# Both convolutions of a four-block network: TensorE reads the centre operand in place from X, 192 elements from column to column

## The chip, the cores and the metric

The kernel runs on one core of one Trainium2 chip. The metric is the device time of one execution in microseconds; before the change its median is 4312.59 us over 3 runs (4307.71 to 4313.99).

## The reference

The input is 2 images of 192 channels and 112 x 112 pixels in float32. Four blocks follow one another: window attention with an MLP; a Sobel filter with a 1x1 fusion, a norm over channels and a GELU; a block with a depthwise 7x7 convolution, a norm, an MLP of 768 hidden features with response normalisation, and a residual; and a sum of seven depthwise convolutions, some dilated, each with its batch norm. The kernel folds the last block into one depthwise 13x13 convolution with a bias. The change touches the two depthwise convolutions alone:

```python
# block 3, first step
y = conv_general_dilated(x, dw_w, padding=((3, 3), (3, 3)), feature_group_count=192) + dw_b
# block 4
out = bn(dwconv(x, w_lk, 1))
for i, (w, r) in enumerate(zip(branch_ws, (1, 1, 2, 3, 4, 5))):
    out = out + bn(dwconv(x, w, r))
```

## The kernel before

The whole activation lives in one on-chip tensor `X` of shape [128, NB = 196, C = 192]. A partition is a position in a patch of 8 rows by 16 columns of pixels; the 196 blocks are 2 images x 14 x 7 such patches; the channel is the innermost index. So for a fixed channel the 196 values of a partition lie 192 elements, 768 bytes, apart.

`depthwise` runs twice: as `dw7` after the Sobel stage and as `dw13` at the end. It loops over the 192 channels. For a channel, the convolution becomes matmuls whose stationary operand is a 128 x 128 Toeplitz matrix of taps (`mats`), and whose moving operand is the channel's blocks, one column for each block. A pixel's neighbours lie in its own patch or in patches around it. Six matmuls add up in one PSUM bank: for each of the row offsets 0, -1 and +1 one with the centre operand and one with the operand shifted by half a patch. Offset 0 has 196 columns, the others 182.

Five engines work on a channel, coupled by semaphores and rings of R = 4 buffers:

- SP loads the channel's taps, spread out, from DRAM into `raw` (line 1145, ring of U = 8).
- VectorE (`body`, up to line 1182) waits until the matmuls of four channels before have freed the ring place (`conv`), copies X's channel into the dense tile `xc` (line 1179, signals `xc_ready`), waits for `raw`, and copies it into the first Toeplitz matrix (line 1182, `mats_a`).
- GpSimd copies the shifted operand `xs` in two halves from X, 64 partitions and 168 elements each (line 1165, `xs_ready`).
- ScalarE writes the second Toeplitz matrix (line 1196, `mats_b`) and, two channels behind, adds the bias and moves the result out of PSUM (line 1209): in dw7 back into X at the same channel, in dw13 into a dense tile `res` that a DMA from ScalarE's queue stores.
- TensorE waits for the operands and for the PSUM bank, and issues the six matmuls (line 1232).

`run_steps` writes the first 8 channels out with constant addresses and runs the other 184 in a loop of 8 channels a turn, whose channel number comes from a register. The order on each engine is that of the program; there is no planner.

Of the kernel before, what the change touches and what calls it, by code (L numbers as in the profile page):

```python
# [23 lines left out]
IMG, BY, BX = 2, 14, 7  # L24
# [1085 lines left out]
def depthwise(nc, tag, turn, q, loaded, wide, bias, X, PS, out, expanded, stack):  # L1110
# [4 lines left out]
    s = Scope(nc, tag, stack)  # L1115
    U, HEAD, R, G = 8, 8, 4, 4
    raw = s.sb("raw", [128, U, RUN[turn]])
    mats = s.sb("mats", [128, R, 2, 24, 16])
    xc = s.sb("xc", [128, R, IMG, BY, BX])
    xs = s.sb("xs", [128, R, IMG * BY, BX])  # L1120
    brow = s.sb("brow", [128, C])
    res = s.sb("res", [128, 2, G, NB]) if out is not None else None
# [10 lines left out]
    with nc.Block() as block:  # L1133
        @block.sync
        def _(sp):
            sp.dma_start(brow[:, :], bias.partition_broadcast(128)).then_inc(q["bloaded"], 16)  # L1136
            sp.wait_ge(expanded, 16 * EXPANSIONS)

            def body(t):
                b = t.ahead(first)  # L1140
                if t.reached(U):
                    sp.wait_ge(q["mats_a"], b.n - U + 1)
                    sp.wait_ge(q["mats_b"], b.n - U + 1)
                src = wide[bass.ds(t.n, 1)].rearrange("o p g -> (o p) g")
                sp.dma_start(raw[:, b.buf(U), :], src).then_inc(loaded[b.buf(U)], 16)
            run_steps(sp, C, U, HEAD, 0, body)

        @block.gpsimd
        def _(pool):
            nc.gpsimd.memset(mats[:, :, :, :, :], 0.0).then_inc(q["cleared"], 1)  # L1150
            nc.gpsimd.memset(xs[:, :, :, :], 0.0).then_inc(q["ready"], 1)
            pool.wait_ge(q["ready"], turn + 1)

            def body(t):
                b = t.ahead(first)
                reached = at_hand(pool, b.n - R + 1)
                pool.wait_ge(q["ready"], turn + 1)
                if b.reached(R):
                    pool.wait_ge(q["conv"], reached)
                for h in range(2):  # L1160
                    if h:
                        pool.wait_ge(q["xs_half"], b.n + 1)
                    src = X[64 * h:64 * h + 64, :, bass.ds(t.n, 1)].rearrange("p (y x) o -> p y (x o)", x=BX)
                    dst = xs[64 * h:64 * h + 64, b.buf(R), :, :]
                    last = nc.gpsimd.tensor_copy(dst[:, :, h:h + BX - 1], src[:, :, 1 - h:BX - h])  # L1165
                    if not h:
                        last.then_inc(q["xs_half"], 1)
                last.then_inc(q["xs_ready"], 1)
            run_steps(pool, C, U, HEAD, 0, body)

        @block.vector
        def _(dve):
            dve.wait_ge(q["cleared"], turn + 1)

            def body(t):
                b = t.ahead(first)
                if b.reached(R):
                    dve.wait_ge(q["conv"], b.n - R + 1)
                nc.vector.tensor_copy(xc[:, b.buf(R)].rearrange("p i y x -> p (i y x)"), X[:, :, bass.ds(t.n, 1)].rearrange("p b o -> p (b o)"))\  # L1179
                    .then_inc(q["xc_ready"], 1)  # L1180
                dve.wait_ge(loaded[b.buf(U)], b.turn(U) * 16 + 16)
                nc.vector.tensor_copy(mats[:, b.buf(R), 0, held, :], toeplitz(b, 0)).then_inc(q["mats_a"], 1)  # L1182
            run_steps(dve, C, U, HEAD, 0, body)

        @block.scalar
        def _(act):
            act.wait_ge(q["bloaded"], 16 * (turn + 1))
            act.wait_ge(q["cleared"], turn + 1)

            def body(t):  # L1190
                if t.inside(C):
                    b = t.ahead(first)
                    if b.reached(R):
                        act.wait_ge(q["conv"], b.n - R + 1)
                    act.wait_ge(loaded[b.buf(U)], b.turn(U) * 16 + 16)  # L1195
                    nc.scalar.activation(mats[:, b.buf(R), 1, held, :], toeplitz(b, 1), ACT.Identity).then_inc(q["mats_b"], 1)  # L1196
                c = t.back(2)
                if not c.inside(C):
                    return
                b = c.ahead(first)  # L1200
                act.wait_ge(q["conv"], b.n + 1)
                src = PS[:, b.buf(4), 0:NB]
                if out is None:
                    dst = X[:, :, bass.ds(c.n, 1)].rearrange("p b o -> p (b o)")
                else:
                    dst = res[:, c.buf(2 * G) // G, c.buf(G), :]
                    if c.reached(2 * G) and c.buf(G) == 0:
                        act.wait_ge(stored[c.buf(2 * G) // G], c.turn(2 * G) * 16)
                nc.scalar.activation(dst, src, ACT.Identity, bias=brow[:, bass.ds(c.n, 1)]).then_inc(q["result"], 1)  # L1209
                if out is not None and c.buf(G) == G - 1:  # L1210
                    act.wait_ge(q["result"], b.n + 1)
                    act.dma_start(out[bass.ds(c.n - (G - 1), G)].rearrange("c p b -> p c b"), res[:, c.buf(2 * G) // G]).then_inc(stored[c.buf(2 * G) // G], 16)
            run_steps(act, C, U, HEAD, 2, body)
            if out is not None:
                for j in range(2):
                    act.wait_ge(stored[j], 16 * (C // G // 2))

        @block.tensor
        def _(pe):
            def body(t):  # L1220
                b = t.ahead(first)
                pe.wait_ge(q["xc_ready"], b.n + 1)
                pe.wait_ge(q["xs_ready"], b.n + 1)
                pe.wait_ge(q["mats_a"], b.n + 1)
                pe.wait_ge(q["mats_b"], b.n + 1)
                if b.reached(4):
                    pe.wait_ge(q["result"], b.n - 3)
                src = (xc[:, b.buf(R)], xs[:, b.buf(R)].rearrange("p (i y) x -> p i y x", i=IMG))
                for i, (oy, sh) in enumerate(((0, 0), (0, 1), (-1, 0), (-1, 1), (1, 0), (1, 1))):
                    ylo, yhi = max(0, -oy), BY - max(0, oy)  # L1230
                    m = mats[:, b.buf(R), sh, 8 * (1 - oy):8 * (1 - oy) + 8, :].rearrange("p r c -> p (r c)")
                    last = nc.tensor.matmul(ps(b)[:, :, ylo:yhi, :], m, src[sh][:, :, ylo + oy:yhi + oy, :], start=(i == 0), stop=(i == 5))  # L1232
                last.then_inc(q["conv"], 1)
            run_steps(pe, C, U, HEAD, 0, body)
# [233 lines left out]
def build(nc, a, out):  # L1468
# [10 lines left out]
    with ExitStack() as whole:  # L1479
        whole.enter_context(nc.allow_non_contiguous_dma(reason="vectors of 192 to 768 elements, once"))  # L1480
        X = whole.enter_context(nc.sbuf_tensor("X", [128, NB, C], F32))
        PS = whole.enter_context(nc.psum_tensor("PS", [128, 8, 512], F32))
        expanded = nc.alloc_semaphore("expanded")
        used = nc.snapshot_sems()
        with ExitStack() as stack:
            attention(nc, a, d, X, PS, expanded, stack)
        nc.clear_and_free_semaphores(nc.allocated_since(used))
        nc.all_engine_barrier()
        with ExitStack() as stack:
            mlp(nc, a, d, X, PS, stack)  # L1490
        with ExitStack() as stack:
            sobel(nc, a, d, X, PS, stack)
        sems = Scope(nc, "dw", whole)
        convs = ({x: sems.sem(x) for x in ("bloaded", "ready", "cleared", "mats_a", "mats_b", "xc_ready", "xs_half", "xs_ready", "conv", "result")},
                 sems.sems("loaded", 8))
        with ExitStack() as stack:
            depthwise(nc, "dw7", 0, *convs, d["wide"][0], a["L2_conv_dw_b"], X, PS, None, expanded, stack)
        with ExitStack() as both:
            gain2 = both.enter_context(nc.sbuf_tensor("gain2", [128, IMG, MC, C], F32))
            cvec = both.enter_context(nc.sbuf_tensor("cvec", [128, C], F32))  # L1500
            with nc.sbuf_tensor("ss", [128, NP, MC], F32) as ss:
                with ExitStack() as stack:
                    hidden(nc, a, d, X, PS, ss, stack)
                with ExitStack() as stack:
                    response_norm(nc, a, PS, ss, gain2, cvec, stack)
            with ExitStack() as stack:
                project(nc, a, d, X, PS, gain2, cvec, stack)
        with ExitStack() as stack:
            depthwise(nc, "dw13", 1, *convs, d["wide"][1], d["bias"], X, PS, out, expanded, stack)
# [25 lines left out]
```

## Time and profile before

| what | value |
|---|---|
| median of 3 runs | 4312.59 us |
| the profiled execution | 4318.69 us, its span 4316.8 us |
| mean granted TensorE clock | 0.93 of full speed |
| PE busy | 3693.2 us (86%) |
| VectorE, ScalarE, GpSimd busy | 55%, 42%, 44% |
| dw7's matmuls (line 1232) | from 2749.8 us to about 3117 us |
| dw13's matmuls | from 3945.2 us to the end |

Busy times are summed over the span and hide that the stages differ; slices and windows split them. Two consecutive matmul records overlap in the trace, so the printed duration of one is longer than the distance to the next. In a timeline "x2" means that two records in a row have been put on one line. The column after the second "|" in the groups is the idle time of the engine before the group, with what ended it.

### The profile page before, as it was taken

How to read it: one execution, taken by the hardware profiler on the slowest of the kernel's cores; microseconds unless marked ns; L12 is line 12 of the kernel's file. 1: busy time of each engine (PE TensorE's matmuls, PEld its weight loads, DVE VectorE, ACT ScalarE, POOL GpSimd, SP SyncE). 2: the span in 40 equal slices, each digit the busy share in tenths (PEclk: the TensorE clock that was granted, in tenths of full speed). 3: DMA queues.
4: the chain of work that ended last, by engine and by line, in shares of the span. 5: the costliest groups of instructions: out<-in, count | busy, mean ns of one | idle time of the engine just before them, and what ended most of it. 6: DMA issues, size and time to landing. Idle time of an engine off the chain costs nothing. (4 is left out here: it accounts for less than half of the span.)

```text
span 4316.8 us, 104641 instructions
## 1 busy us (share of the span) xinstructions
PE 3693.2 (86%) x32726; PEld 3544.2 (82%) x32726; DVE 2377.2 (55%) x5922; ACT 1823.7 (42%) x5208; POOL 1902.3 (44%) x2891
## 2 busy tenths in 40 slices
PE   3888888888869999999755555699999989999999
PEld 2777777777769999999755555699989989999999
DVE  2555555556543333333399999544389971113444
ACT  1555555555534444444211122344379960001444
POOL 2222222222213333333499999555434433334555
PEclk9999999989979999999877777899999999999999
DMA  2444566620000000000122322455457778887887
GB/s 62 137 160 161 176 221 211 219 86 19 19 19 20 21 27 27 23 24 27 45 60 75 79 72 72 125 149 149 114 163 199 199 197 253 253 252 241 266 267 228
DMA packets 473876, 551.74 MB, mean 128 GB/s; under 512 B 89875, under 2 KB 343573, under 8 KB 473621
## 3 DMA queue, kind: packets, MB, share of 16 engines
q1 hardware_dynamic: 448276, 528.61, 41.6%
q10 hardware_dynamic: 25344, 19.27, 1.4%
q8 instruction: 216, 3.54, 0.3%
q14 instruction: 40, 0.32, 0.0%
HBM read 408.63 MB, written 271.27 MB: 158 GB/s over the span
## 5 line engine op out<-in xcount | busy, mean ns | idle before, releaser
L1232 PE MATMUL PS<-dw_xc,dw_mats 128*128 128x182 f32 (+1 forms) x2304 | 554.4, 322 | 34.4 <-ACT dw_mats L1196 34.4
L1104 PE MATMUL PS<-sobel_wf,sobel_edge 96*128 96x192 f32 (+1 forms) x1568 | 333.2, 384 | 268.6 <-DVE sobel_edge L1035 234.2
L1165 POOL COPY dw_xs<-X 64x168 f32 (+1 forms) x768 | 426.4, 555 | 300.5 <-PE PS L1232 238.8
L1232 PE MATMUL PS<-dw_xs,dw_mats 128*128 128x182 f32 (+1 forms) x2304 | 553.3, 321 | 0.0
L1104 PEld LDWEIGHTS PS<-sobel_wf,sobel_edge 96*128 96x128 f32 (+1 forms) x1568 | 325.1, 232 | 276.6 <-issue 261.7
L1232 PEld LDWEIGHTS PS<-dw_xc,dw_mats 128*128 128x128 f32 x2304 | 401.5, 190 | 35.0 <-issue 35.0
L880 PE MATMUL PS<-mlp_w,mlp_hid 128*128 128x192 f32 x2352 | 414.2, 326 | 0.5 <-ACT mlp_hid L756 0.5
L1232 PEld LDWEIGHTS PS<-dw_xs,dw_mats 128*128 128x128 f32 x2304 | 401.1, 189 | 0.0
L362 POOL TENSOR_SCALAR att_ve<-att_mv 128x2 f32<-128x2 f32 x98 | 22.5, 229 | 858.9 <-DVE att_mv L409 858.9
L1463 PE MATMUL PS<-gain,down_hid 128*128 128x192 f32 x2352 | 385.5, 328 | 3.8 <-DMA down_hid<-scratch_hid 3.8
L1463 PEld LDWEIGHTS PS<-gain,down_hid 128*128 128x128 f32 x2352 | 385.2, 191 | 4.2 <-DMA down_hid<-scratch_hid 4.2
L880 PEld LDWEIGHTS PS<-mlp_w,mlp_hid 128*128 128x128 f32 x2352 | 378.7, 190 | 0.8 <-ACT mlp_hid L756 0.8
L1179 DVE COPY dw_xc<-X 128x196 f32 (+1 forms) x384 | 149.1, 388 | 392.6 <-PE PS L1232 383.0
L1196 ACT ACTIVATE dw_mats<-dw_raw 128x224 f32<-128x224 f32 (+1 forms) x384 | 163.7, 426 | 453.2 <-DMA dw_raw<-scratch_wide 422.9
L487 ACT ACTIVATE att_vbd<-PS 64x96 f32<-64x96 f32 x784 | 194.7, 248 | 341.7 <-PE PS L596 334.9
L840 DVE TENSOR_TENSOR mlp_x<-PS,X 128x192 f32<-128x192 f32 x196 | 70.2, 358 | 482.0 <-PE PS L880 472.6
L756 ACT ACTIVATE mlp_hid<-PS,mlp_b 128x256 f32<-128x256 f32 x588 | 247.0, 471 | 111.0 <-PE PS L747 111.0
L807 POOL COPY X<-mlp_x 128x192 f32 (+1 forms) x196 | 68.2, 348 | 468.5 <-DVE mlp_x L840 467.5
L756 ACT ACTIVATE hid_hid<-PS,hid_b 128x256 f32<-128x256 f32 x588 | 236.9, 471 | 34.2 <-PE PS L747 34.2
L1451 DVE TENSOR_TENSOR X<-PS,down_x 128x192 f32 (+1 forms) x196 | 70.0, 357 | 319.5 <-PE PS L1463 319.5
L1443 POOL TENSOR_TENSOR down_x<-down_x,cvec 128x192 f32<-128x192 f32 x196 | 115.8, 591 | 271.9 <-DMA down_x<-scratch_x 271.9
L1182 DVE COPY dw_mats<-dw_raw 128x224 f32<-128x224 f32 (+1 forms) x384 | 223.8, 583 | 3.9 <-DMA dw_raw<-scratch_wide 3.6
(218 smaller groups left out, 10379.9 us busy)
## 6 DMA issues: line engine op xcount, KB each, us to landing
scratch_wide<-scratch_taps SPq DMA_DIRECT2D x64, 1188.0 KB, 6.6
dw_raw<-scratch_wide SPq DMA_DIRECT2D x192, 396.0 KB, 4.1
scratch_hid<-hid_hid SPq DMA_DIRECT2D x196, 384.0 KB, 3.6
down_hid<-scratch_hid SPq DMA_DIRECT2D x196, 384.0 KB, 4.1
scratch_wide<-scratch_taps SPq DMA_DIRECT2D x64, 828.0 KB, 5.1
dw_raw<-scratch_wide SPq DMA_DIRECT2D x192, 276.0 KB, 2.8
sobel_xin<-scratch_x SPq DMA_DIRECT2D x56, 420.0 KB, 3.9
att_x<-in_x SPq DMA_DIRECT2D x196, 96.0 KB, 1.9
```

What stands on the lines that cost most here:

```text
L487: last = nc.scalar.activation(vbd[64 * e:64 * e + 64, b.buf(4), w, :, e, 0:HD], src, ACT.Identity)
L756: last = nc.scalar.activation(hid[:, m, :], self.psU[i][:, e * 256:(e + 1) * 256], ACT.Gelu, bias=self.b1[:, m:m + 1])
L840: nc.vector.tensor_tensor(x1[:, b.buf(2), :], psD[b.buf(2)], at(X, b.n), ALU.add).then_inc(q["x1_ready"], 1)
L880: last = nc.tensor.matmul(psD[i], hid[:, p.buf(2), m, i * 128:(i + 1) * 128], w2[:, m, :], start=(m == 0), stop=(m == MC - 1))
L1104: last = nc.tensor.matmul(psF(t, j), edge[0:rows, t.buf(2), e, j, :], wf[0:rows, e, :], start=(e == 0), stop=(e == 2 * KC - 1))
L1165: last = nc.gpsimd.tensor_copy(dst[:, :, h:h + BX - 1], src[:, :, 1 - h:BX - h])
L1179: nc.vector.tensor_copy(xc[:, b.buf(R)].rearrange("p i y x -> p (i y x)"), X[:, :, bass.ds(t.n, 1)].rearrange("p b o -> p (b o)"))\
L1182: nc.vector.tensor_copy(mats[:, b.buf(R), 0, held, :], toeplitz(b, 0)).then_inc(q["mats_a"], 1)
L1196: nc.scalar.activation(mats[:, b.buf(R), 1, held, :], toeplitz(b, 1), ACT.Identity).then_inc(q["mats_b"], 1)
L1232: last = nc.tensor.matmul(ps(b)[:, :, ylo:yhi, :], m, src[sh][:, :, ylo + oy:yhi + oy, :], start=(i == 0), stop=(i == 5))
L1443: nc.gpsimd.tensor_tensor(x2[:, b.buf(R), :], x2[:, b.buf(R), :], cvec[:, :], ALU.add).then_inc(q["resid"], 1)
L1463: last = nc.tensor.matmul(PS[:, b.buf(R), 0:C], hid[:, b.buf(R), m, :], gain2[:, img, m, :], start=(m == 0), stop=(m == MC - 1))
```

## The change

The tile `xc`, VectorE's copy into it and its semaphore are dropped. The moving operand of the three centre matmuls becomes a view of X itself at the channel, in dw7 and dw13 alike. The shifted operand, the Toeplitz matrices, the order of the matmuls and their number of columns stay as they are.

```diff
-    xc = s.sb("xc", [128, R, IMG, BY, BX])
...
                 if b.reached(R):
                     dve.wait_ge(q["conv"], b.n - R + 1)
-                nc.vector.tensor_copy(xc[:, b.buf(R)].rearrange("p i y x -> p (i y x)"), X[:, :, bass.ds(t.n, 1)].rearrange("p b o -> p (b o)"))\
-                    .then_inc(q["xc_ready"], 1)
                 dve.wait_ge(loaded[b.buf(U)], b.turn(U) * 16 + 16)
...
-                pe.wait_ge(q["xc_ready"], b.n + 1)
                 pe.wait_ge(q["xs_ready"], b.n + 1)
...
-                src = (xc[:, b.buf(R)], xs[:, b.buf(R)].rearrange("p (i y) x -> p i y x", i=IMG))
+                centre = X[:, :, bass.ds(t.n, 1)].rearrange("p (i y x) o -> p i y (x o)", i=IMG, y=BY)
+                src = (centre, xs[:, b.buf(R)].rearrange("p (i y) x -> p i y x", i=IMG))
                 for i, (oy, sh) in enumerate(((0, 0), (0, 1), (-1, 0), (-1, 1), (1, 0), (1, 1))):
```

`"xc_ready"` also leaves the list of semaphores in `build`.

## Rows read from the trace of the kernel before

**Rows 1.** Busy us, share and instructions by engine, from the page.
```profile
PE 3693.2 (86%) x32726; PEld 3544.2 (82%) x32726; DVE 2377.2 (55%) x5922; ACT 1823.7 (42%) x5208; POOL 1902.3 (44%) x2891
```

**Rows 2.** The span in 40 slices of 107.9 us, from the page.
```profile
PE   3888888888869999999755555699999989999999
...
PEclk9999999989979999999877777899999999999999
```

**Rows 3.** Windows: us; busy us (count) PE, PEld, DVE, ACT, POOL; clock, DMA, GB/s.
```profile
2775.00:2950.00 175.00, 175.00 (x1108) 175.00 (x1108) 79.47 (x186) 74.30 (x186) 102.41 (x185) 1.00 0.55 149
3945.00:4312.80 367.80, 367.53 (x2304) 367.28 (x2304) 173.89 (x382) 157.18 (x383) 211.16 (x380) 0.99 0.86 260
```

**Rows 4.** Chain that ended last, in order: start us, us, what.
```profile
3939.27 5.14 DMA dw_raw<-scratch_wide
...
3944.51 0.48 ACT dw_mats L1196
...
3945.23 367.54 PE PS L1232 x2304
```

**Rows 5.** Waits in the first convolution: us in total, times, longest.
```profile
DVE dw_xc L1179 <- PE PS L1232: 98.6, 95, 1.0
```

**Rows 6.** Timeline of one channel: start us, us, engine, line, operation, count.
```profile
3002.01 0.49 PE L1232 MATMUL PS<-dw_xc,dw_mats 128*128 128x196 f32 x2
...
3003.30 0.47 PE L1232 MATMUL PS<-dw_xc,dw_mats 128*128 128x182 f32 x2
...
3003.61 0.47 PE L1232 MATMUL PS<-dw_xs,dw_mats 128*128 128x182 f32 x2
...
3003.91 0.49 PE L1232 MATMUL PS<-dw_xc,dw_mats 128*128 128x196 f32 x2
```

**Rows 7.** Groups by line and shape: count, busy us, mean ns.
```profile
L1232 PE MATMUL PS<-dw_xc,dw_mats 128*128 128x182 f32 x1536 | 363.7, 318 | 0.0
```

**Rows 8.** VectorE's two copies: duration ns min/median/max.
```profile
L1179 DVE COPY dw_xc<-X x384: 364/384/770, 2746.9 to 4305.3; 128x196 f32 x184, 128x196 f32<-128x196 f32 x8
...
L1182 DVE COPY dw_mats<-dw_raw x384: 277/569/626, 2749.2 to 4305.6; 128x224 f32<-128x224 f32 x96, 128x320 f32<-128x320 f32 x96
```

**Rows 9.** GpSimd's shifted copy and its register operations, as rows 8.
```profile
L1165 POOL COPY dw_xs<-X x768: 451/477/705, 2747.6 to 4306.2; 64x168 f32 x184, 64x168 f32<-64x168 f32 x8
L1165 POOLq FUSED_REGOPS  x736: 42/46/56, 2761.3 to 4306.1; - x184
```

**Rows 10.** ScalarE's groups, as rows 7: strided, dense, two dense sizes.
```profile
L1209 ACT ACTIVATE X<-PS,dw_brow 128x196 f32 x184 | 111.0, 603 | 201.8 <-PE PS L1232 201.8
...
L1196 ACT ACTIVATE dw_mats<-dw_raw 128x320 f32<-128x320 f32 x192 | 89.0, 464 | 441.9 <-DMA dw_raw<-scratch_wide 411.7 <-ACT dw_res L1209 30.2
...
L1209 ACT ACTIVATE dw_res<-PS,dw_brow 128x196 f32<-128x196 f32 x192 | 81.5, 424 | 179.4 <-PE PS L1232 179.4
...
L1196 ACT ACTIVATE dw_mats<-dw_raw 128x224 f32<-128x224 f32 x192 | 74.7, 389 | 11.2 <-DMA dw_raw<-scratch_wide 11.2
```

**Rows 11.** A dense GpSimd copy, as rows 8.
```profile
L807 POOL COPY X<-mlp_x x196: 342/349/500, 1303.9 to 2120.2; 128x192 f32 x168, 128x192 f32<-128x192 f32 x28
```

**Rows 12.** GpSimd's groups, as rows 7: shifted copy, 6-element copy.
```profile
L1165 POOL COPY dw_xs<-X 64x168 f32 x736 | 409.3, 556 | 289.4 <-PE PS L1232 229.3 <-POOL dw_xs L1165 60.1
...
L1275 POOL COPY ss<-hid_part 128x6 f32 x90 | 17.1, 190 | 120.5 <-DVE hid_squares L1304 120.5
```

**Rows 13.** Timeline of line 747, PE alone, first and last of 14 records.
```profile
3399.73 0.28 PE L747 MATMUL PS<-hid_ha_hi,hid_wa_lo 128*128 128x256 f32 x1
...
3401.24 0.28 PE L747 MATMUL PS<-hid_hb,hid_wb_lo 128*128 128x256 f32 x1
```

**Rows 14.** Timeline of the first convolution's first channel, PE alone.
```profile
2751.24 0.81 PE L1232 MATMUL PS<-dw_xc,dw_mats 128*128 128x182 f32 x2
2751.85 0.81 PE L1232 MATMUL PS<-dw_xs,dw_mats 128*128 128x182 f32 x2
```

**Rows 15.** Window of the stretch of rows 14, columns as rows 3.
```profile
2751.20:2753.00 1.80, 1.80 (x7) 1.80 (x7) 0.84 (x3) 0.00 (x0) 1.16 (x2) 0.50 1.04 406
```

More of the change, by code:

```diff
@@ L1493, in build @@
         sems = Scope(nc, "dw", whole)
-        convs = ({x: sems.sem(x) for x in ("bloaded", "ready", "cleared", "mats_a", "mats_b", "xc_ready", "xs_half", "xs_ready", "conv", "result")},
+        convs = ({x: sems.sem(x) for x in ("bloaded", "ready", "cleared", "mats_a", "mats_b", "xs_half", "xs_ready", "conv", "result")},
                  sems.sems("loaded", 8))
```

## The prediction

> **What bounds the kernel now.** I read first the busy shares of the page: PE is busy 86% of the span, its weight loads (PEld, which overlap) 82%, and no other engine is above 55% [rows 1]. An average over stages says little, so the slices come next: PE stands at 9 in the slices near 2750 to 3113 us and in those from 3945 us to the end, the two convolutions, with PEclk 9 [rows 2]. The windows table makes it exact: in 175 us of the first convolution PE is busy for 175.00 us at granted clock 1.00, while VectorE is busy 79, ScalarE 74 and GpSimd 102 us; the second shows 367.53 of 367.80 us [rows 3]. The chain that ended last agrees: from 3945.23 on it is 367.54 us of line 1232 [rows 4]. The waits show the other side: VectorE's xc copy waits for PE, 98.6 us in 95 times in a like window [rows 5]. Last, the timeline of one channel: centre and shifted matmuls alternate, and a channel takes from 3002.01 to 3003.91, 1.90 us [rows 6]. So TensorE alone sets the pace of both convolutions, and what counts is how long its own matmuls take.
>
> **How the program's matmuls stand in the trace.** A channel has 6 matmuls, 3 of them on the centre operand. Two of the 3 have 182 columns, over 384 channels 768, and the trace has 1536 records of them [rows 7]: each f32 matmul is two records, each with all its columns. A printed duration (318 ns) is not a record's cost, since they overlap; the cost is the spacing. 1108 records in 175 us [rows 3] are 0.158 us each, 12 a channel, 1.895 us. With 186.7 columns in the mean that is 0.85 ns a column. The centre reads per channel are 2 x (196 + 182 + 182) = 1120 columns.
>
> **The change part by part.**
>
> *The copy goes.* 384 copies of 384 ns [rows 8], about 149 us of VectorE. Each begins when PE has freed its ring place and has 98.6/95 = 1.04 us of idle VectorE in front of it [rows 5]; it lies wholly beside the PE of a channel. Worth 0 us. What PE still needs, the shifted copies and both Toeplitz copies, is made up to three channels ahead and comes as early as before or earlier, so nothing is late in its place.
>
> *One wait goes* in front of PE's channel. The spacing from a channel's last pair to the next channel's first is 0.30 to 0.31 us, that inside a channel 0.31 [rows 6]: the five waits that are there now cost nothing visible. I take 0; a bound for the gain is 0.01 us x 384 = 4 us. At the start of each convolution PE's first matmul waits for ScalarE's Toeplitz copy, whose data came by DMA [rows 4], not for xc: 0.
>
> *Addresses from a register.* For 184 of 192 channels the centre matmuls' addresses now depend on the loop counter. The trace shows what that costs GpSimd: one FUSED_REGOPS of 46 ns for each copy of X [rows 9]. PE's form is not shown. If each of the 6 centre records needs one, 6 x 46 = 276 ns of issuing stand beside 1895 ns of streaming and run ahead of it, since the ring has operands ready. I take 0; uncovered, it is 0.276 x 368 = 102 us.
>
> *The read itself.* This is the term that decides. The moving operand was dense in xc; now its consecutive columns lie 192 x 4 = 768 bytes apart. No row shows PE reading so. The nearest rows are of other engines doing the very same walk over X. ScalarE, from the same PSUM source with the same 196 elements, takes 603 ns to write to X and 424 ns to write densely [rows 10]: +179 ns, 0.91 ns an element. Its dense pace is (464 - 389)/(320 - 224) = 0.78 ns [rows 10], so 1.69 ns an element with the step. GpSimd reads X: its dense copy takes 349 ns for 192 elements and 190 for 6, 0.85 ns an element [rows 11, 12]; with the step the median is 477 ns for 168 [rows 9], (477 - 190)/162 = 1.77 ns. VectorE's copy has 384 ns for 196, its dense Toeplitz copy at its quickest 277 for 224 [rows 8]: at least 107 ns more for fewer elements, 0.55 ns each. Three engines, reads and writes, each lose 0.5 to 0.9 ns where neighbours are 768 bytes apart, and two end at 1.7 to 1.8 ns an element. That looks like the pace of the memory for lone words, and PE needs one every 0.85 ns.
> I take 1.69 ns, because its pair of rows differs in nothing but the step. Then a centre column costs 1.69 - 0.85 = 0.84 ns more: 1120 x 0.84 = 0.94 us a channel, 361 us over 384. Low end: nothing, if PE's port has room (below). A gain is excluded, since the columns are the same and there was no gap to close. High end: GpSimd's mean beside other traffic, 556 ns [rows 12], is (556 - 190)/162 = 2.26 ns, so 1.41 x 1120 x 384 = 606 us.
>
> *A rule against the change.* What the rows show is the loss of 0.5 to 0.9 ns an element [rows 8 to 12]. The Trainium skill, "SBUF — State Buffer", section "SBUF: two separate sides", says that the memory is read in lines of 16 bytes and that two hits on a line are needed to hide its latency; "Advanced Engine Details and Errata", "SBUF Cachelines", says that a new line at each access is penalised. By that rule each column of X is a line of its own and the change loses; the three engines of this trace agree in sign. "Vector Engine (DVE) Microarchitecture Reference", "Measured stream behaviour on trn2", gives 0.65 of a VectorE cycle for each lone word, about 0.68 ns; as an estimate from that page the sum would be 1120 x 0.68 x 384 = 292 us. Neither page gives a number for TensorE, and no row here does.
>
> *Sum.* The profiled execution took 4318.7 us (span 4316.8 us, 1.9 us around it), 6.1 us above the median of the runs, 4312.6. On its time: 4318.7 + 361 = 4680; on the median 4674. I put the forecast at 4676. What else touches the time: with a channel of 2.84 us the other engines have more slack; their longest here, GpSimd, is busy 102 of 175 us.
>
> **The rivals.**
>
> *A. The step is free for PE* (not slower). PE's own moving operand is read faster elsewhere: the single-record matmuls of line 747 start 1.51/13 = 0.116 us apart with 256 columns [rows 13], 0.454 ns a column of 4 bytes. An f32 record takes only one column per 0.85 ns. If the step halves that rate, PE gets one per 0.91 ns, which is 0.06 ns late: 1120 x 0.06 x 384 = 26 us at most, and 0 if the 0.454 ns hold some cost per record. Time 4310 to 4340, likeliest 4313. For it: PE can take nearly double what an f32 record asks, while the engines above were at their own pace when dense. Against it: the 0.454 ns is for neighbours side by side, as was ScalarE's 0.78, and that one didn't save ScalarE from 1.69 with the step. It decides if a lone word comes in 0.85 ns or less.
>
> *B. Each record reads each column twice.* 0.85 ns is nearly twice 0.454 ns, so a record may fetch a column for each of two passes. At 1.69 ns a fetch a column takes 3.38 ns: 2.53 x 1120 x 384 = 1088 us, 5400 us. Against it: two passes could use one fetch.
>
> *C. Issuing decides.* The 102 us above in full, with a free read: 4415 us. The first 8 channels of each convolution, whose addresses are constants, would keep 1.895 us while the others don't.
>
> *D. A smaller loss for the step*, by buffering in front of the array: 50 to 230 us, 4360 to 4545.
>
> *E. Faster*: waits gone and one reader of X fewer, at most the 4 us above, 4309; over 0.2% would need something that no row shows.
>
> **How the numbers follow.** Forecast (1.4 to 1.8 ns a column, 4550 to 4760 around 4676): 0.52. A: 0.26. B and other losses above 4770, among them a granted clock that falls while the array is fed slowly (at the lower clock a pair of 182 columns takes 0.61 us, at the full one 0.31 [rows 6, 14, 15]): 0.09. C: 0.03. D: 0.07. E: 0.03. The predicted time is the likeliest, 4676. A has to be inside, so the range runs from 4306 to 4770 and leaves out B and a corner; the forecast's own is 4550 to 4760. What can be told from no change is about 0.2%, 9 us. Of A's 0.26, 0.04 may lie above that. Faster 0.03, same 0.22, slower 0.75.
>
> **What the profile after would show.** The spacing of the line 1232 records that read X against those that read xs is the whole test: about 0.33 us a record of 196 columns under the forecast, 0.165 under A, 0.66 under B; the shifted records keep 0.158. Under the forecast a channel takes 2.84 us, PE still waits for nobody, the idle time in front of ScalarE's activations grows by nearly 1 us, and the second convolution goes from 367.5 us to about 548. VectorE loses 149 us of busy time in every case. All other stages keep their times. The forecast is wrong if the records on X keep the spacing of the others, if only the loop's channels are longer (C), or if the clock falls in the convolutions.

## The result and the profile after

The changed kernel takes 4670.69 us (median of 4 runs, 4665.56 to 4675.08) against 4310.15 us for the kernel before (4 runs): a ratio of 1.0843, 95% interval 1.0813 to 1.0873. It is 360.5 us slower. The forecast was 4676, 5 us above the measured time.

The page's first lines, busy us and instructions by engine, answer to [rows 1]:
```profile
PE 4050.7 (87%) x32726; PEld 3650.3 (78%) x32726; DVE 2153.6 (46%) x5538; ACT 1826.9 (39%) x5208; POOL 1845.5 (39%) x2891
```
PE's busy time grew by 357 us with the same 32726 records. VectorE's fell by 224 us.

A window in the first convolution, columns as [rows 3]:
```profile
2775.00:2950.00 175.00, 175.00 (x739) 134.44 (x738) 17.18 (x62) 51.12 (x124) 59.71 (x124) 1.00 0.36 100
```
A channel has 12 records. 739 records in 175.00 us are 12 in 2.842 us, where [rows 3] gave 1.895. PE is still busy throughout, and its weight loads now have gaps. The chain that ended last (start us, us, what) has the same content as [rows 4], only longer:
```profile
4121.54 547.81 PE PS L1229 x2304
...
4669.37 0.42 ACT dw_res L1206
```
547.81 us for 367.54 us, +180.3. The first convolution, from its first matmul to the end of its last result (2742.2 to 3290.2 + 0.65, below; before 2749.8 to 3116.7), went from 366.9 to 548.7 us, +181.8. Its start lay 7.6 us earlier, a difference that had come about before the change's first instruction. 180.3 + 181.8 - 7.6 is 354.5 of the 356.4 us between the two spans. ScalarE's activations of line 1206 (before: line 1209), ns min/median/max, first and last start:
```profile
L1206 ACT ACTIVATE X<-PS,dw_brow x192: 587/641/674, 2746.3 to 3290.2; 128x196 f32 x184, 128x196 f32<-128x196 f32 x8
```
One channel on PE, the counterpart of [rows 6]:
```profile
3102.14 0.82 PE L1229 MATMUL PS<-X,dw_mats 128*128 x2
3102.79 0.51 PE L1229 MATMUL PS<-dw_xs,dw_mats 128*128 128x196 f32 x2
3103.14 0.78 PE L1229 MATMUL PS<-X,dw_mats 128*128 x2
3103.74 0.49 PE L1229 MATMUL PS<-dw_xs,dw_mats 128*128 128x182 f32 x2
3104.06 0.78 PE L1229 MATMUL PS<-X,dw_mats 128*128 x2
3104.66 0.49 PE L1229 MATMUL PS<-dw_xs,dw_mats 128*128 128x182 f32 x2
3104.99 0.49 PE L1229 MATMUL PS<-X,dw_mats 128*128 x1
```
The pair on X of 182 columns lasts from 3103.14 to 3103.74, 0.60 us, the shifted pair behind it 0.32. Before, each had 0.31. The three centre pairs of this channel take 1.85 us together, where they took 0.95, and the three shifted ones 1.00 for 0.95. So nearly all of the loss stands in the centre pairs, and about 0.05 us of the 0.95 us shows in the shifted pairs behind them. The waits have the same form as [rows 5], and none of them is PE's:
```profile
DVE dw_mats L1179 <- PE PS L1229: 159.3, 62, 2.7
ACT X L1206 <- PE PS L1229: 125.3, 62, 2.1
```
ScalarE now waits 125.3/62 = 2.02 us for PE in front of each result. Before, in the view of [rows 5], it was 104.0/95 = 1.09:
```profile
ACT X L1209 <- PE PS L1232: 104.0, 95, 1.1
```

Two more places help to decide between reasons. The first eight channels have constant addresses:
```profile
2753.09 0.78 PE L1229 MATMUL PS<-X,dw_mats 128*128 128x182 f32 x2
2753.69 0.49 PE L1229 MATMUL PS<-dw_xs,dw_mats 128*128 128x182 f32 x2
2754.01 0.78 PE L1229 MATMUL PS<-X,dw_mats 128*128 128x182 f32 x2
```
0.60 us again (2753.09 to 2753.69), so the register address is not the cause. The other channels show what TensorE's register addresses need:
```profile
L1229 PEldq FUSED_REGOPS  x736: 42/46/51, 2762.7 to 4664.1; - x184
```
That is two operations of 46 ns for each of the 368 channels in the loops, 92 ns a channel. And the first channel, at the low clock; the window of its middle has a granted clock of 0.50:
```profile
2743.63:2745.47 1.84, 1.84 (x7) 1.84 (x7) 0.67 (x1) 0.00 (x0) 0.56 (x1) 0.50 1.05 407
```
```profile
2743.63 0.81 PE L1229 MATMUL PS<-X,dw_mats 128*128 128x182 f32 x2
2744.26 0.80 PE L1229 MATMUL PS<-dw_xs,dw_mats 128*128 128x182 f32 x2
2744.85 0.82 PE L1229 MATMUL PS<-X,dw_mats 128*128 128x182 f32 x2
2745.47 0.80 PE L1229 MATMUL PS<-dw_xs,dw_mats 128*128 128x182 f32 x2
2746.06 0.86 PE L1229 MATMUL PS<-X,dw_mats 128*128 128x196 f32 x2
```
Here the X pairs take 0.63 and 0.62 us and the shifted ones 0.59, where [rows 14] had 0.61 for a dense centre pair. At the low clock the step costs 0.01 to 0.02 us a pair, at the full clock 0.29. A pair on X takes about the same time at both clocks, as if it were bound by something that doesn't run with PE's clock.

### The profile page after: what moved, and what is told of

It is laid out like the page before. It is cut to its first block and busy times, and to the rows that moved or that the text cites. A ratio compares the mean times of both kernels' runs of the same rounds, so it can differ in the third digit from the quotient of the medians.

```text
span 4673.2 us, 104886 instructions
## 1 busy us (share of the span) xinstructions
PE 4050.7 (87%) x32726; PEld 3650.3 (78%) x32726; DVE 2153.6 (46%) x5538; ACT 1826.9 (39%) x5208; POOL 1845.5 (39%) x2891
## 5 line engine op out<-in xcount | busy, mean ns | idle before, releaser
L1229 PE MATMUL PS<-X,dw_mats 128*128 (+2 forms) x2304 | 912.8, 485 | 33.8 <-ACT dw_mats L1193 26.4
L1229 PEld LDWEIGHTS PS<-dw_xs,dw_mats 128*128 128x128 f32 x2304 | 477.7, 207 | 251.3
L1164 POOL COPY dw_xs<-X 64x168 f32 (+1 forms) x768 | 372.9, 485 | 708.7 <-PE PS L1229 647.1
L1229 PE MATMUL PS<-dw_xs,dw_mats 128*128 128x182 f32 (+1 forms) x2304 | 574.1, 330 | 0.0
L1179 DVE COPY dw_mats<-dw_raw 128x224 f32<-128x224 f32 (+1 forms) x384 | 116.6, 304 | 973.7 <-PE PS L1229 955.3
L1229 PEld LDWEIGHTS PS<-X,dw_mats 128*128 128x128 f32 x2304 | 400.5, 189 | 34.3 <-POOL dw_xs L1164 34.3
L1206 ACT ACTIVATE X<-PS,dw_brow 128x196 f32 (+1 forms) x192 | 121.2, 631 | 389.7 <-PE PS L1229 389.7
L1206 ACT ACTIVATE dw_res<-PS,dw_brow 128x196 f32<-128x196 f32 x192 | 81.3, 424 | 359.6 <-PE PS L1229 359.6
```

## The experiments

All are edits of the kernel before. What a column costs in a centre record is worked out as in the prediction: the channel's time, less 0.948 us for the shifted half (half of 1.895), over 1120 columns (560 where a centre matmul is one record). This puts on the centre what the shifted pairs lose too: for X it gives 1.691 ns, while the spacing of the centre pairs alone is 1.85/1120 = 1.65 ns. A "lone word" is a column of 4 bytes with no neighbour next to it or in the same line. Single executions of the kernel before range from 4295 to 4325 us, so where a run was timed only once, its window carries the reading and not the time.

### The other half of the change alone

```diff
+            nc.vector.memset(xc[:, :, :, :, :], 1.0).then_inc(q["xc_ready"], 1)
...
-                nc.vector.tensor_copy(xc[:, b.buf(R)]..., X[:, :, bass.ds(t.n, 1)]...).then_inc(q["xc_ready"], 1)
...
+            pe.wait_ge(q["xc_ready"], turn + 1)         # once, ahead of the loop
...
-                pe.wait_ge(q["xc_ready"], b.n + 1)
```

> The other half of the change alone: the dense tile xc is filled once with ones, VectorE's 384 copies and the wait per channel are gone, and TensorE still reads dense (the centre part is computed from ones). My theory, that all of the loss is in the stepped read and the copy lay beside TensorE's work: the time of before, within 4 us (4306 to 4313 on 4310), a channel 1.895 us. Rival, that the copy's going is worth something by itself and the stepped read hides part of it: 10 us or more below before.

4309.15 us (12 runs) against 4309.73 for the kernel before (22 runs), ratio 0.9994, interval 0.998 to 1.0007. The window of the first convolution:
```profile
2775.00:2950.00 175.00, 175.00 (x1109) 175.00 (x1108) 25.48 (x92) 73.83 (x186) 86.44 (x186) 1.00 0.55 149
```
1109 records for 1108. The copy and the wait were worth nothing that the interval can tell from zero (at most some 9 us), while VectorE's busy time in the window fell from 79.47 to 25.48 us. So all of the 360 us belongs to the stepped read.

### One convolution alone

```diff
                 src = (xc[:, b.buf(R)], xs[:, b.buf(R)]...)
+                if turn:
+                    src = (X[:, :, bass.ds(t.n, 1)]..., src[1])
```

> Only the second convolution reads X in place; there nobody writes X. Theory: the second convolution takes 548 us as in the changed kernel, the first 364 us as before; 180 us of the 360, 4490 us. Rival, that ScalarE's writes into X beside TensorE's reads (first convolution only) make part of the loss: the second convolution would already have shown it by a shorter channel, so the total would stand under 4480.

4487.75 us (4 runs, beside the same 4309.73), ratio 1.042, interval 1.0395 to 1.0445: 178 us. The chain of the second convolution:
```profile
3933.37 547.98 PE PS L1235 x2304
```
547.98 us, though nobody writes X there and VectorE still makes its copy. ScalarE's writes into X and the missing copy have no part in it.

### A step inside the dense tile

```diff
-    xc = s.sb("xc", [128, R, IMG, BY, BX])
+    xc = s.sb("xc", [128, R, NB, S])          # S = 2, 3, 4; 8 in the first convolution only
...
-    ...tensor_copy(xc[:, b.buf(R)]..., X[...])
+    ...tensor_copy(xc[:, b.buf(R), :, 0], X[...])
...
-                src = (xc[:, b.buf(R)], ...)
+                src = (xc[:, b.buf(R), :, 0]..., ...)
```

> xc stays with its copy and constant addresses, but each element stands in a slot of 2: TensorE reads with a step of 8 bytes, nothing from X. If 8 bytes is the unit (neighbours in pairs): every word is alone, centre pairs of 182 columns take 0.60 us, 4670 us. If lines of 16 bytes with two hits are enough: dense pace, 0.31 us, 4310 us. Rival, that the tile X or the address from a register is the cause: 4310 us too.

> As the step of 2, with a slot of 4 elements: a step of 16 bytes, every word in a 16-byte line of its own. Theory (a lone word per fetch costs 1.65 to 1.69 ns wherever it lies): centre pairs of 182 columns take 0.60 us, 4670 us. Rival, that it is X, its traffic, the register address or the size of the 768-byte step: 4310 us.

> A step of 3 elements (12 bytes) in both convolutions: four columns lie in three or four 16-byte lines, at every fourth column two neighbours share one. If the price is per line touched (1.69 to 1.77 ns for each line, 0.85 dense): 3/4 of it, 1.27 to 1.33 ns a column, a channel 0.95 + 1.45 = 2.4 us, 4500 us. If anything over 8 bytes is a lone word: 1.7 ns, 2.85 to 2.93 us a channel, 4680 to 4710 us. If the step's size alone counted below 16 bytes: dense, 1.9 us.

> As the run with a step of 4 elements, with 8 (32 bytes), in the first convolution only. The step of 16 bytes cost 1.77 ns a column per record, X's 768 bytes 1.69 ns. If nearness of the lines makes the difference: between the two or 1.69 ns, a channel of 2.84 to 2.93 us. If the tile xc or VectorE's writing beside it does: 1.77 ns, 2.93 us, as with 4.

Windows of the first convolution, in the order of steps of 8, 12, 16 and 32 bytes:
```profile
2775.00:2950.00 175.00, 175.00 (x1080) 175.00 (x1079) 77.73 (x180) 72.33 (x180) 99.89 (x181) 1.00 0.53 145
```
```profile
2775.00:2950.00 175.00, 175.00 (x863) 152.98 (x862) 61.73 (x143) 57.32 (x143) 79.86 (x144) 1.00 0.42 115
```
```profile
2775.00:2950.00 175.00, 175.00 (x717) 130.94 (x716) 52.13 (x120) 48.43 (x120) 67.07 (x120) 1.00 0.35 96
```
```profile
2775.00:2950.00 175.00, 175.00 (x709) 129.54 (x708) 51.15 (x118) 47.66 (x118) 66.03 (x118) 1.00 0.35 95
```
The counts give channels of 1.944, 2.433, 2.929 and 2.962 us. In time: the step of 2 took 4325.63 us (7 runs, ratio 1.0033, interval 1.0013 to 1.0053), the step of 4 4707.39 us (2 runs, 1.0925, 1.0892 to 1.0958), the step of 3 4514.13 us and the step of 8, in one convolution, 4519.7 us (one run each, beside 4302.87 for before). The step of 4 came out 37 us above the 4670 that I expected, since a column took 1.769 ns and not 1.65 to 1.69. So a step of 16 bytes in a tile of its own, with constant ring addresses, costs at least what the in-place read costs, 398 us for 360: X, its traffic, the register and the 768 bytes are all cleared. The step of 8 bytes is nearly free, against the reading that the unit is 8 bytes. The step of 12 bytes, four columns in three lines, takes three quarters: 1.326 ns a column against 1.769, as the price per line forecast. The step of 8 elements failed my expectation: if nearness of the lines made the difference, it had to lie between 1.77 and X's 1.69, and it is 1.80.

### Pairs of neighbours in X

```diff
+                    if turn and sh == 0:
+                        last = nc.tensor.matmul(PS[:, b.buf(4), 0:cols]..., m, X[:, 0:cols // 2, bass.ds(first_ch, 2)], ...)
+                        continue
```

> Second convolution only, in place from X, but two neighbouring channels (2k, 2k+1) of each of half as many blocks, so as many columns, in pairs that start on 8 bytes, 768 bytes from pair to pair (the centre part is computed from those values). If the cost is that of a fetch per lone word and a fetch brings two neighbours: dense pace, second convolution 368 us, 4310 us. If it is the distance of 768 bytes, the tile X or the register address: 548 us, 4490 us.

> As the run before, but pairs that start on an odd word: channels 8k+1 and 8k+5 (inside a 16-byte line) for six of eight channels, 8k+3 (across two lines) for two of eight. If the unit is 16 bytes: the six at dense pace, pair of 182 columns 0.31 us, the two at 0.60 us; second convolution about 413 us. If the unit is 8 bytes: all eight at 0.60 us, 548 us.

Even pairs, then odd pairs, in the second convolution:
```profile
3990.00:4290.00 300.00, 300.00 (x1892) 300.00 (x1892) 146.69 (x316) 129.73 (x315) 181.10 (x315) 1.00 0.89 266
```
```profile
3990.00:4290.00 300.00, 300.00 (x1687) 277.14 (x1687) 134.47 (x282) 116.08 (x282) 166.94 (x281) 1.00 0.80 237
```
The second convolution took 368.5 us with the even pairs, for 368 expected, and 413.6 us with the odd ones, for 413 (the whole runs 4317.61 and 4342.34 us, once each, beside 4302.89). Even pairs: 12 records in 1.903 us, dense pace, though from pair to pair it is 768 bytes, X is read in place and the address comes from a register. Odd pairs: a mean of 2.134 us. The timeline shows what it is a mean of; it begins inside the second channel whose pairs lie across two lines:
```profile
4105.23 0.78 PE L1235 MATMUL PS<-X,dw_mats 128*128 x2
4105.83 0.49 PE L1237 MATMUL PS<-dw_xs,dw_mats 128*128 128x182 f32 x2
4106.15 0.49 PE L1235 MATMUL PS<-X,dw_mats 128*128 x2
4106.49 0.49 PE L1237 MATMUL PS<-dw_xs,dw_mats 128*128 128x196 f32 x2
4106.82 0.47 PE L1235 MATMUL PS<-X,dw_mats 128*128 x2
4107.13 0.47 PE L1237 MATMUL PS<-dw_xs,dw_mats 128*128 128x182 f32 x2
4107.44 0.47 PE L1235 MATMUL PS<-X,dw_mats 128*128 x2
```
0.60 us for the pair of 182 columns at 4105.23; from 4106.15 on, where both words lie in one 16-byte line though on an odd word, 0.34 for 196 and 0.31 for 182. (6 x 1.90 + 2 x 2.845)/8 = 2.136 us is the measured mean. So for these two-record matmuls what counts is how many columns in a row come from one line of 16 bytes.

### Centre matmuls of one record

```diff
+    matr = s.sb("matr", [128, R, 24, 16], F32R)
-    xc = s.sb("xc", [128, R, IMG, BY, BX])
+    xc = s.sb("xc", [128, R, NB, S], F32R)    # S = 1; 2; 4 in the first convolution only
...
+                    if sh == 0:
+                        last = nc.tensor.matmul(PS[:, b.buf(4), 0:cols], matr..., xc[:, b.buf(R), 0:cols, 0], ...)
+                        continue
```
For the last of the four, xc is [128, R, NB // 2, 4] and the columns are read as [0:cols // 2, 0:2].

> The three centre matmuls of both convolutions in the single-record type (fp32r, rounded operands, columns taken in plain order), dense: the base for the next run. One record per matmul at 0.454 ns a column: 0.083 us for 182 columns between the neighbouring shifted pairs. TensorE needs 1.2 us a channel, so another engine (GpSimd, 1.1 to 1.3 us) may set the pace of the channel; what counts is the distance of the records inside a channel.

> The same with a step of 16 bytes in the first convolution. If a lone word has a pace of its own (a floor, 1.65 to 1.75 ns a column): 0.30 to 0.32 us for 182 columns. Rival, that the step adds about 0.85 to 0.9 ns to whatever a column takes (my additive bound): 0.454 + 0.88 = 1.33 ns, 0.24 us. Rival, that a two-record matmul fetches twice within a record and a single one once: half of the floor, 0.15 us.

> The single-record centre matmuls with a step of 8 bytes in both convolutions. With 16 bytes they took 0.90 ns a column. If one 16-byte line can come every 0.85 to 0.9 ns and two columns share a line: 0.45 ns a column, which the dense run does too, so its channel of 1.28 us. If a single record pays for any step: up to 1.45 us.

> Single-record centre matmuls, columns in adjacent pairs, pair from pair 16 bytes away, first convolution only. The single-record type paid the same 0.89 to 0.90 ns a column at steps of 8 and 16 bytes. If it takes two columns at a time and pays when the two are not neighbours: the dense run's channel, 1.28 us. If instead each 16-byte line costs 1.77 ns in this type too (two columns a line at a step of 8 bytes give 0.89): 0.89 ns a column again, 1.45 us.

Windows in the order dense, 16 bytes, 8 bytes, pairs 16 bytes apart:
```profile
2775.00:2950.00 175.00, 175.00 (x1230) 175.00 (x1228) 117.56 (x273) 109.45 (x273) 144.30 (x273) 1.00 0.80 220
```
```profile
2775.00:2950.00 175.00, 175.00 (x1083) 175.00 (x1082) 104.74 (x242) 97.24 (x241) 135.21 (x241) 1.00 0.74 194
```
```profile
2775.00:2950.00 175.00, 175.00 (x1090) 175.00 (x1089) 105.09 (x242) 97.83 (x242) 135.65 (x242) 1.00 0.74 195
```
```profile
2775.00:2950.00 175.00, 175.00 (x1090) 175.00 (x1089) 104.94 (x242) 97.77 (x242) 135.04 (x242) 1.00 0.74 195
```
A channel has 9 records: 1.280, 1.454, 1.445 and 1.445 us. The whole runs took 4086.58, 4116.38 and 4131.99 us beside 4302.89, 4302.89 and 4302.87 for before, and 4109.43 beside 4313.15, once each; the steps of the second and the fourth stand in the first convolution only. Dense, that leaves at most 0.593 ns a column, more than line 747's 0.454 [rows 13]; with 182 columns the run does not show the read's own pace, since the weight loads run without a gap too. As soon as the columns are not all neighbours it is 0.89 to 0.90 ns, if the shifted half costs 0.948 us here as well. The timeline of the 16-byte run can't show that it does:
```profile
2900.61 0.45 PE L1237 MATMUL PS<-dw_xc,dw_matr 128*128 128x182 f32 x1
2900.88 0.49 PE L1239 MATMUL PS<-dw_xs,dw_mats 128*128 128x182 f32 x2
2901.08 0.47 PE L1237 MATMUL PS<-dw_xc,dw_matr 128*128 128x196 f32 x1
```
The next centre record starts 0.20 us after the first of a shifted pair, for 0.31 in the kernel before, so the starts no longer divide the channel between the halves. If the shifted half costs what line 747's 0.454 ns leaves it in the dense run, 1.280 - 560 x 0.454 = 1.026 us, the stepped columns take 0.75 to 0.76 ns. These are estimates, and the figures of 0.89 and 0.90 are to be read as upper ends. The floor of 1.65 to 1.75 ns a lone word, my theory, is refuted for this type, and so is the additive bound of 1.33; what was measured is about half the floor, as the third reading had it. That the steps of 8 and 16 bytes cost the same, and that the pairs cost it too, against the reading that this type takes two neighbours at a time, is what "a line of 16 bytes every 1.77 ns" gives for two columns a line, but not for one.

## Why the prediction came out right

**The bound.** TensorE set the pace of both convolutions and still does. Confirmed by the windows, and by the run without the copy.

**The copy and the wait, 0 us.** Shown: the ratio is 0.9994. Its interval alone would still allow 9 us, more than my bound of 4; the window is sharper, with 1109 records for 1108.

**Addresses from a register, 0 us.** The eight channels with constant addresses have the same 0.60 us, and the even pairs in X, with a register address, keep the dense pace. The six operations of 46 ns a channel were a guess; the trace has two, 92 ns. Rival C is out. With 360.5 us the total lies outside D's 50 to 230 us and E's gain as well.

**The read, 0.84 ns a column, 361 us.** The size held: (2.842 - 0.948)/1120 = 1.691 ns a column, for which I took 1.69, and 360.5 us for 361. That the size was right does not make its reason right. I read 1.7 ns as the memory's pace for a lone word, from ScalarE and GpSimd. For two-record matmuls this describes what happens, in any tile. But a single record takes lone words at 0.90 ns or less, so it is no pace of the memory as such. The agreement with ScalarE's 1.69 ns, to the last digit, was in part luck. ScalarE's pair of rows does not differ "in nothing but the step": one is from the first convolution and one from the second, both are writes, and the dense pace of 0.78 ns comes from copies of another tile. And the centre pairs' own spacing is 1.65 ns, the rest being the shifted pairs' 0.05 us.

The forecast's own upper end does not follow from its figures: 1.8 ns a column is 0.95 x 1120 x 384 = 409 us, 4721 us, and 4760 would need 1.89 ns. The result doesn't hang on it.

**Rivals A and B.** A said that the step would halve PE's best rate, from 0.454 to 0.91 ns; for single records the runs show about that, 0.76 to 0.90. It gave 26 us because it took one fetch for each column of an f32 record. B said two fetches, but at 1.69 ns each. Halved rate times two fetches is 1.8 ns, near the 1.69 to 1.80 of the lone words. This table holds what was measured; a line's time is the column's times the columns in it.

| record | columns lie | columns per 16-byte line | ns a column | ns a line |
|---|---|---|---|---|
| f32, two records | dense | 4 | 0.846 | 3.38 |
| | 8 bytes apart | 2 | 0.890 | 1.78 |
| | pairs in X, in one line | 2 | 0.853 | 1.71 |
| | 12 bytes apart | 4 in 3 | 1.326 | 1.77 |
| | 16 bytes apart | 1 | 1.769 | 1.77 |
| | 32 bytes apart | 1 | 1.798 | 1.80 |
| | X, 768 bytes | 1 | 1.691 | 1.69 |
| single record | dense (line 747) | 4 | 0.454 | 1.82 |
| | 8 bytes apart, or pairs | 2 | 0.75 to 0.887 | 1.50 to 1.77 |
| | 16 bytes apart | 1 | 0.76 to 0.904 | 0.76 to 0.90 |

With the upper ends, every row but the last fits "a new line no sooner than 1.7 to 1.8 ns". All rows fit if an f32 record asks for each column twice, and a line costs 0.9 ns when asked once, 1.7 to 1.8 when asked two to four times, and 3.4 when asked eight times. That it asks twice is inferred from this table and not shown; that the single type reads in another way would do as well. This stays open. It does not touch the sum of this change.

The Trainium skill's "SBUF — State Buffer", section "SBUF: two separate sides", wants two hits on a 16-byte line. For f32 matmuls the runs agree: 0.890 and 0.853 ns with two, 1.69 to 1.80 with one. For single records they don't: two columns a line cost 0.75 to 0.887 for 0.454 ns. The rule of the Trainium skill's "Vector Engine (DVE) Microarchitecture Reference", section "Measured stream behaviour on trn2", full rate for adjacent pairs of 4-byte words that start on 8 bytes, does not carry over to TensorE's f32 matmuls: words 8 bytes apart and pairs on an odd word inside a line are at or near dense pace. The estimate of 292 us from that page was 68 us short.

**VectorE's busy time.** "Loses 149 us in every case" was wrong: it lost 224. The Toeplitz copies went from 583 to 304 ns in the mean, 107 us over 384, now that they start ahead of GpSimd's copy of X (below). With the 149 us of the xc copies that is 256 us of durations, but 224 of busy time, in which overlapping instructions count once: before, a Toeplitz copy was started some 0.09 us before the xc copy's end. The step that failed took the copies to be independent. VectorE does not set the pace, so this had no price.

## What to carry to other kernels

Before an operand of an f32 matmul is read in place, count how many consecutive columns come from one 16-byte line: with one, the matmul took twice as long here; with two, also in pairs far apart, it is all but free. A copy on an engine with slack that packs the operand is then free as long as TensorE sets the pace. Ask of every copy that seems superfluous what layout it makes, since removing it moves its cost to whoever reads next. And when a size comes out right, test the reason too: here the right size came with a reason that single records refuted.

## What the runs showed that I had not expected

VectorE's and GpSimd's copies can slow each other where they run side by side. In the kernel before, VectorE's dense Toeplitz copy has a median of 569 ns [rows 8]; without the xc copy it starts earlier, ahead of GpSimd's, and for 224 elements takes 279 ns (mean), for 558 before; some 0.09 us of the 558 is the overlap with the xc copy. The groups of the run without the copy, columns as [rows 7]:
```profile
L1165 POOL COPY dw_xs<-X 64x168 f32 x736 | 347.0, 471 | 351.5 <-PE PS L1232 291.5 <-POOL dw_xs L1165 60.1
...
L1181 DVE COPY dw_mats<-dw_raw 128x224 f32<-128x224 f32 x192 | 53.5, 279 | 308.5 <-PE PS L1232 306.3 <-DMA dw_raw<-scratch_wide 2.1
```
GpSimd's shifted copy gains as well, 471 ns for 556 [rows 12]. That it is GpSimd's copy, and not VectorE's own copy in front, is seen in the changed kernel, which has no xc copy. There one Toeplitz copy of the first channels happened to start just behind GpSimd's and took 670 ns:
```profile
2743.65 0.56 POOL L1164 COPY dw_xs<-X 64x168 f32<-64x168 f32 x1
2743.67 0.67 DVE L1179 COPY dw_mats<-dw_raw 128x224 f32<-128x224 f32 x1 [0.41 <-DMA dw_raw<-scratch_wide]
```
Other copies in the same stretch overlap GpSimd's and still take 278 ns, so overlap alone doesn't decide. What does is open. This has no price here, for neither sets the pace; it would where one of them does.

X is also slightly cheaper for TensorE than the spread-out tiles: 1.69 ns a column at 768 bytes, 1.77 at 16 and 1.80 at 32. It is not that farther lines are cheaper, since 32 bytes cost more than 16. It is not the missing copy either: in the run with one convolution, where VectorE still copies, the second convolution takes the same 548 us. Why is open.
